# Eight of the 416 row gathers of the last pass issued row by row from the sync engine

## The reference

```
def _L3_gnn_ref(h, weight, edge_src, edge_dst, edge_rel, edge_norm):
    msg = h[edge_src] * edge_norm[:, None]
    seg = edge_rel * N + edge_dst
    agg = jax.ops.segment_sum(msg, seg, num_segments=R * N)
    agg = agg.reshape(R, N, NUM_BASES, SUBMAT_IN)
    W = weight.reshape(R, NUM_BASES, SUBMAT_IN, SUBMAT_OUT)
    out = jnp.einsum('rnbi,rbio->nbo', agg, W)
    return out.reshape(N, NUM_BASES * SUBMAT_OUT)
...
x = _layernorm(x + _L3_gnn_ref(x, L3_gnn_weight, src, dst, edge_type_8, edge_weight), axis=-1)
```

## Time and profile before

| | us |
|---|---|
| runs of the kernel before | 3873.62, 3883.31, 3894.91 |
| median | 3883.31 |
| span of the profiled execution, first to last instruction | 3344.4 |
| median less that span | 538.9 |
| start of the relation pass in the span | 2801 |
| end of its last gather's issue, of the span | 3322.7, 3344.4 |

### The profile page before, as it was taken

One profiled execution on the slowest core, in us unless ns is written; L12 is line 12 of the kernel. 1 busy time (PEld: TensorE's weight loads), 2 busy tenths in 40 slices (PEclk: granted clock), 3 DMA queues, 4 the chain that ended last, 5 costly groups with the idle time before them and its releaser, 6 DMA issues. The chain is left out here.

```text
span 3344.4 us, 57629 instructions
## 1 busy us (share of the span) xinstructions
PE 2832.4 (85%) x14883; PEld 1787.6 (53%) x14883; DVE 2497.0 (75%) x6123; ACT 1941.1 (58%) x6302; POOL 2174.9 (65%) x2298
## 2 busy tenths in 40 slices
PE   5799889999989799588888785899999897888786
PEld 5666555555556455355555453666666653333333
DVE  8899789999977555599999753799988874444444
ACT  1478645555542354399999821788888753333334
POOL 4777667777767542677777465777766314777775
PEclk9999889999999899699999987899999996655655
DMA  6234488888871588887877655778777444333335
GB/s 198 93 98 129 124 247 263 263 263 262 263 192 34 162 324 345 283 255 244 245 236 237 170 175 185 230 236 236 235 214 225 114 194 171 105 105 106 105 105 118
DMA packets 260608, 651.27 MB, mean 195 GB/s; under 512 B 66797, under 2 KB 115642, under 8 KB 253514
## 3 DMA queue, kind: packets, MB, share of 16 engines
q0 software_dynamic: 141840, 474.50, 46.7%
q1 hardware_dynamic: 118458, 173.08, 15.8%
HBM read 505.42 MB, written 145.27 MB: 195 GB/s over the span
## 5 line engine op out<-in xcount | busy, mean ns | idle before, releaser
L2155 POOL DMA_INDIRECT a_rows<-table,met x568 | 544.3, 958 | 216.5 <-issue 153.7
L3754 PE MATMUL ps<-rows_in,hot_w 128*128 128x256 f32 x832 | 440.9, 642 | 96.0 <-ACT hot_w L3722 58.7
L1354 POOL DMA_INDIRECT rows_in<-table,met x416 | 413.4, 994 | 142.0 <-issue 80.0
L3696 POOL DMA_INDIRECT rows_in<-table,met x416 | 394.5, 948 | 144.2 <-issue 119.5
L3800 DVE TENSOR_TENSOR xs<-xs,ps 128x256 f32 x416 | 175.0, 421 | 283.9 <-PE ps L3754 279.2
L3754 PEld LDWEIGHTS ps<-rows_in,hot_w 128*128 128x128 f32 x832 | 196.5, 289 | 340.4 <-ACT hot_w L3722 191.0
L3722 ACT ACTIVATE hot_w<-hot,met 128x128 f32<-128x128 f32 x416 | 166.6, 401 | 355.5 <-PE ps L3754 338.4
L2634 PE MATMUL ps<-a_rows,a_hot 128*128 128x260 f32 x1136 | 317.9, 408 | 20.2 <-DVE acc L2640 16.3
L2640 DVE TENSOR_TENSOR acc<-acc,ps 128x520 f32 x416 | 286.1, 688 | 42.9 <-PE ps L2634 34.1
L857 POOL DMA_INDIRECT records<-rec,rows x241 | 260.2, 1080 | 82.5 <-issue 72.9
L2155 POOL DMA_INDIRECT xs<-table,met x264 | 252.5, 957 | 93.7 <-issue 71.0
(11 more groups left out here) (488 smaller groups left out, 6290.5 us busy)
## 6 DMA issues: line engine op xcount, KB each, us to landing
a_hot_t<-one_hots SPq DMA_DIRECT2D x104, 256.0 KB, 5.5
table<-stage SPq DMA_DIRECT2D x25, 1024.0 KB, 3.8
rows_in<-table,met POOLq DMA_INDIRECT x832, 3.8
one_hots<-hot_t SPq DMA_DIRECT2D x52, 256.0 KB
dst_row<-slot_rows SPq DMA_DIRECT2D x51, 256.0 KB, 5.0
by_dst<-dst_rows SPq DMA_DIRECT2D x25, 512.0 KB
by_dst<-lo_rows SPq DMA_DIRECT2D x24, 512.0 KB
a_rows<-table,met POOLq DMA_INDIRECT x568, 4.0
```

The costliest lines, as they stand in the source:

```text
L1354: e.indirect_dma_start(self.rows[:, n % self.RING, 0:2 * D], None, self.table, bass.IndirectOffsetOnAxis(ap=self.b.met[:, n, R_SRC:R_SRC + ...
L2155: e.indirect_dma_start(self.row(n, 0, self.width), None, self.table, bass.IndirectOffsetOnAxis(ap=b.met[:, n, self.word:self.word + 1], ax ...
L3696: e.indirect_dma_start(self.rows[:, n % self.RING, :], None, self.table, bass.IndirectOffsetOnAxis(ap=self.b.met[:, n, R_REL:R_REL + 1], a ...
L3754: e.matmul(b.ps[:, n % self.BANKS, 0:D], self.hot_w[:, n % GRP_H, :], self.rows[:, n % self.RING, :], start=True, stop=True).then_inc(self ...
```

## The change

Of the 416 chunks eight, the numbers 49, 99, 149 and so on to 399 (`by_side`), are no longer gathered by GpSimd. The other 408 (`by_pool`) keep their gather, with the ring slot counted over these alone. For the eight, SP writes their 1024 row numbers from SBUF to DRAM in chunk order, reads them back into one partition, and then, eight rows at a time, loads eight numbers into registers and issues eight transfers, each of one row of 1 KB whose DRAM address comes from a register. The rows go to `side_rows`, two chunks deep: from the third on SP waits until TensorE has multiplied the chunk two before. TensorE takes the rows of these chunks from `side_rows`, after waiting for all 128 transfers. The stores of the result come behind all this in SP's list.

```diff
+    EVERY, SIDE = 50, 8
+    PER_LOAD = 8
...
+        self.by_side = [self.EVERY * (j + 1) - 1 for j in range(self.SIDE)]
+        self.by_pool = [n for n in range(NCH) if n not in self.by_side]
+        self.side_rows, self.side_ids = sb("side_rows3", [P, 2, D]), sb("side_ids3", [1, self.SIDE, P], I32)
+        self.ids_dram = b.dram("side_ids", [self.SIDE, P], I32)
+        self.ids_put, self.ids_back = b.counted("load_3", 16), b.counted("load_4", 16)
+        self.side_arrived = [b.counted(f"load_{h + 1}", 16 * P * len(range(h, self.SIDE, 2))) for h in range(2)]
...
-        for n in range(NCH):
-            if n >= self.RING and n % GRP_H == 0:
-                e.wait_ge(self.summed, self.c0 + n - self.RING + GRP_H)
-            e.indirect_dma_start(self.rows[:, n % self.RING, :], None, self.table,
+        for k, n in enumerate(self.by_pool):
+            if k >= self.RING and k % GRP_H == 0:
+                e.wait_ge(self.summed, self.c0 + self.by_pool[k - self.RING + GRP_H - 1] + 1)
+            e.indirect_dma_start(self.rows[:, k % self.RING, :], None, self.table,
                                  bass.IndirectOffsetOnAxis(ap=self.b.met[:, n, R_REL:R_REL + 1], axis=0)
-                                 ).then_inc(self.arrived[n % self.RING], 16)
+                                 ).then_inc(self.arrived[k % self.RING], 16)
...
+    def wait_rows(self, e, n):
+
+        if n in self.by_side:
+            j = self.by_side.index(n)
+            e.wait_ge(*self.side_arrived[j % 2].at(16 * P * (j // 2 + 1)))
+        else:
+            k = self.by_pool.index(n)
+            e.wait_ge(self.arrived[k % self.RING], 16 * (self.before[k % self.RING] + k // self.RING + 1))
+
     def sync(self, e):
 
         b = self.b
+        regs = [e.alloc_register(f"sum3_s{j}") for j in range(self.PER_LOAD)]
+        first, last = self.by_side[0], self.by_side[-1]
+        e.dma_start(self.ids_dram.rearrange("j p -> p j"), b.met[:, first:last + 1:self.EVERY, R_REL],
+                    allow_slow_non_contiguous=True).then_inc(self.ids_put.sem, 16)
+        e.wait_ge(*self.ids_put.at(16))
+        e.dma_start(self.side_ids[:, :, :].rearrange("a j p -> a (j p)"),
+                    self.ids_dram.rearrange("(a j) p -> a (j p)", a=1)).then_inc(self.ids_back.sem, 16)
+        e.wait_ge(*self.ids_back.at(16))
+        for j in range(self.SIDE):
+            if j >= 2:
+                e.wait_ge(self.summed, self.c0 + self.by_side[j - 2] + 1)
+            for p0 in range(0, P, self.PER_LOAD):
+                e.load(regs, self.side_ids[0:1, j, p0:p0 + self.PER_LOAD])
+                at = [e.snap(r, min_val=0, max_val=NR * NP - 1) for r in regs]
+                for k in range(self.PER_LOAD):
+                    e.dma_start(self.side_rows[p0 + k:p0 + k + 1, j % 2, :], self.table[bass.ds(at[k], 1), :]
+                                ).then_inc(self.side_arrived[j % 2].sem, 16)
         for g in range(self.GROUPS - 1):
...
             e.wait_ge(self.weighted, self.c0 + n + 1)
-            e.wait_ge(self.arrived[n % self.RING], 16 * (self.before[n % self.RING] + n // self.RING + 1))
+            self.wait_rows(e, n)
...
-            e.matmul(b.ps[:, n % self.BANKS, 0:D], self.hot_w[:, n % GRP_H, :], self.rows[:, n % self.RING, :],
+            e.matmul(b.ps[:, n % self.BANKS, 0:D], self.hot_w[:, n % GRP_H, :], self.rows_of(n),
```

More of the change, by code:

```diff
@@ L3731, in tiles, with rows_of @@
         return self.ENDS[g - 1] if g else 0, self.ENDS[g]
+    def rows_of(self, n):
+        if n in self.by_side:
+            return self.side_rows[:, self.by_side.index(n) % 2, :]
+        return self.rows[:, self.by_pool.index(n) % self.RING, :]
+    def wait_rows(self, e, n):
+        if n in self.by_side:
+            j = self.by_side.index(n)
[3 more added lines that the diff above has]
+            e.wait_ge(self.arrived[k % self.RING], 16 * (self.before[k % self.RING] + k // self.RING + 1))
     def sync(self, e):
         b = self.b
+        regs = [e.alloc_register(f"sum3_s{j}") for j in range(self.PER_LOAD)]
[15 more added lines that the diff above has]
+                                ).then_inc(self.side_arrived[j % 2].sem, 16)
         for g in range(self.GROUPS - 1):
```

## The result

| | us |
|---|---|
| changed kernel, median of 5 runs | 4267.61 (4263.02 to 4274.69) |
| kernel before, median of 5 runs | 3889.61 (3873.62 to 3902.05) |
| ratio, 95% interval | 1.097 (1.0948 to 1.0994) |
| predicted | 3922 (3873 to 4055) |

The account below looks back on a forecast made before the run. GpSimd's gathers were taken to pace the relation pass. SP's late side rows, 1024 t - 493.5 at t = 0.52, add 39 us to the span of 3344.4, giving 3383; with 538.9 around it 3922 us, range 3873 to 4055.

Parts of the forecast that it names:

- What bounds the kernel: Relation pass: GpSimd's gathers, 1.253 us each, pace TensorE, which needs about 1.19 to 1.24 us a chunk.
- the same 538.9 us around it: Outside the profiled span: 538.9 us taken as unchanged and added to the forecast span of 3383.
- The cost of a row, t: SP's time per side row: transfer, register instruction and an eighth of the load, 0.505 summed, taken as 0.52 us.
- The signs that it gave for being wrong: SP's register transfers over 0.4 us, row numbers needing far more than 8 us, or SP waiting for `summed`.
- Ahead of the rows: SP's store of row numbers to DRAM and load back before the side rows: 8 us, within 4 to 20.
- The sum: TensorE's chunk 399 possible at 2811 + 1024 t, before at 3304.5; +39 us at t = 0.52.
- rival A: SP keeps up with the side rows, pass 10 us shorter, 3873; decides at t = 0.482; chance 0.23 (t below 0.50).
- Buffers and rings: Two side buffers and GpSimd's 16-slot ring change nothing; SP loses about 5 us per cycle, chunks come some 4 us later.
- Contention: DMA engines in the pass: 1024 more packets of 1 KB, costed at nothing.
- B: SP's row transfers: a register address is dear, t above 0.65, 4086 or 4188 us; chance 0.15.
- C: Outside the span: SP's 2306 more instruction rows would add 22 us to any case; chance 0.02 on top of rival A.
- D: TensorE's clock might fall with eight waits; changes nothing while SP is late, otherwise gives back some of 10 us; no chance given.

Follow-up runs that it names:

- one_block: Changed kernel with each side chunk fetched by one SP transfer of 128 consecutive rows, not row by row; ratio to the kernel before 0.9959, span 3827.9 us.
- control: The kernel before, unchanged, profiled once more; span 3843.1 us, ratio 1.0006, relation pass 613.2 us.
- act_loads: Changed kernel with GpSimd idle in the pass and ScalarE issuing a plain load of 128 consecutive rows for each of 408 chunks; span 3831.8 us.
- no_gathers: Changed kernel with GpSimd gathering only the first 16 chunks, whose rows TensorE reuses for later ones; SP's 1024 rows took 567 us, 0.554 each.
- pool_direct: Changed kernel with GpSimd issuing a plain transfer of 128 consecutive rows per chunk in place of the gather; span 3832.0 us.

## Why the prediction was wrong

*What bounds the kernel.* The bound was right in the trace that was read, and one_block showed it right by its value: eight gathers less gave 11 us of the pass where 10 were worked out. But that trace was no picture of a timed execution. The step "with the same 538.9 us around it" took time that lies inside the span for time around it. In the control TensorE reaches chunk 399 at 3812.7 - 3229.9 = 582.8 us after the first gather, and the prediction had 503. That gave the change 80 us less room than it had, and made the forecast too slow by 80; this error went against the other one and hid part of it.

*The cost of a row, t.* This is the step that failed, and the larger one. The parts were near: transfer 0.225 where 0.25 was taken, register instruction 0.037 where 0.057 was; a move of 0.029 came on top that the list of instructions does not show, and the load on SP took 0.77. Their sum without gathers is 0.54, forecast 0.52. What was not foreseen is that instructions don't keep their durations beside gathers. With them t was 0.929 on average. Nothing in the trace read showed it, as SP is idle in its pass and the stretches were missing from it; but a maximum of 1.643 us beside a median of 0.526 was there to be asked about, and the range for t was made from kinds of transfer alone. The signs that it gave for being wrong don't catch this either: the median transfer took 0.225 us, under its 0.4, and SP waited for no `summed`.

*Ahead of the rows.* The row numbers took from 3271.3 to 3285.3, 14 us, forecast 8 within 4 to 20.

*The sum*, with what was measured: 14 ahead of the rows, 951 for the rows, 1 for the last to land: TensorE can do chunk 399 at 966 us after the first gather, and the trace has 4239.0 - 3272.0 = 967.0. Less the 582.8 of the control, 384 us, which is the whole loss. The formula was right; t and the base were not. With t at its quiet 0.54 and the true base, the sum would be 14 + 553 + 1 - 583 = -15: by it the rows would have been there in time, and rival A, with a gain of 11, would have won. So by this sum the slowing by gathers is not a part of the loss, it is all of it.

*Buffers and rings.* As predicted SP waited for no `summed`, and GpSimd filled its ring and stood. TensorE's eight waits were 48 to 61 us each, predicted at 4 to 5 a cycle (10 to 15 for the first two).

*Contention* was costed at nothing on the DMA engines, and there it is nothing (act_loads). It was looked for in the wrong place: not between transfers but between a gather and another engine's instruction queue.

*The rivals.* B named a t over 0.65 and put it down to the register address; the size was nearer, the reason wrong, since a transfer with a register address takes 0.225 us. C, instructions costing outside the span, falls with the 538.9. D, the clock, played no part that shows: it was granted 0.60 in this pass and 0.62 in the control's.

What stays open is how a gather holds up other engines' instructions. The runs show that it takes the indirect form on GpSimd and not many bytes, that each instruction is delayed, in steps of 0.7 us, and that it sets in some us after a run of gathers begins. They don't show which resource is shared, nor why one execution in all those profiled was free of them, though its gathers ran unbroken at 1.25 us for 500 us. Nor does any run exclude that the recording of the execution has a part in it. No version here beats both kernels: what is to be won is one_block's 0.4%, and the largest correct piece of it, two chunks, is worth 2.5 us and can't be told from no change.

## What to carry to other kernels

Work moved from GpSimd to an idle queue has to be priced with the gathers that remain running, not from a queue's quiet rows; count its instructions, since each is delayed, and not only its transfers. Before a sum is built on a profile, hold its span against the timed runs: where they differ by a seventh, the profile is of another execution, and a second one is worth more than any row of the first. And a sideways path pays only if it is quicker a unit than what it relieves over the same stretch: here 128 rows took 115 us or more, where the 49 gathers between take 70 in the control (1.42 us each on average) and would take 61 unbroken.

## What the runs showed of the hardware

- Gathers with an index list on GpSimd delay the instructions of other engines. SP's row of 3.25 instructions takes 0.54 us without them, 1.5 to 2.0 on average beside those of the pass and 4.55 when they go out unbroken with all else idle, one instruction every 1.40 us of whatever kind; gathers of 64 bytes a row do it as well (0.91 on average against 0.93), plain transfers from GpSimd at 0.54 us each don't.
- The same holds for the engines that compute: 61 steps of TensorE over 3 us in the control; in no_gathers, pool_direct and act_loads there are none but the eight waits for side rows.
- A transfer of one 1 KB row from SP costs the queue 0.225 us with its address from a register and 0.252 with a fixed one, 0.043 to the next; all 1024 on one queue show no floor of their own down to 0.298 us each.
